# Grouped-query attention: the projections of the following sequence made between the attention groups of the sequence in hand

## The chip, the cores and the metric

The kernel runs on one core of a Trainium2 chip. The metric is the device time of one execution in microseconds (us): 7177.83 us for the kernel before, the median of three runs (7176.45 to 7178.78).

## What is computed

The program is a small two-layer network over x of shape [8, 256, 256] (8 sequences of 256 tokens, 256 channels), in float32. Its stages are a recurrent attention (RWKV7), a feed-forward block with masked attention, a gated linear recurrence, that feed-forward block again, a delta-rule attention with 16 heads, a mixture of experts, **grouped-query attention**, and the mixture of experts again. Only the grouped-query attention changes:

```python
h = layernorm(x)                                   # 8 x 256 x 256
q = h @ Wq + bq                                    # 32 heads of 8
k = h @ Wk + bk ; v = h @ Wv + bv                  # 8 key/value heads of 8
for every head: p = softmax(q k^T / sqrt(8)) ; o = p v      # no mask, 256 x 256 scores
x = x + (o @ Wo + bo)
```

## The kernel before

Each stage is a function. It holds its tiles in SBUF, and one program for each engine (`pe`, `act`, `dve`, `pool`, `sp`), written in the order in which that engine does it. Engines wait for each other by semaphores (`wait_ge`, `then_inc`). A `Block` ends when all its engines have ended it; `s.barrier()` follows, and clears the stage's semaphores. `nc.Fori` is a loop that the engines run on the chip, with one copy of its body in the instruction stream.

`gqa` (L1102) first makes the layer norm of all 2048 tokens into `xn_all` (L1133 to L1149); GpSimd's multiply (L140) is its last step, and VectorE clears `v` beside it (L1148). Then `Fori(0, BATCH)` (L1152) runs eight times, one sequence each, and every pass has these parts:

- **Projections.** TensorE makes the queries (8 tiles of 128x256, L1158, PSUM banks 1 to 4), the keys (2 tiles, L1164, bank 5) and the values (L1170, L1172, bank 6). ScalarE adds the bias and copies queries and keys to `qt` and `kt` (L1187, L1192), VectorE spreads the values into `v` (L1203). TensorE waits for all three before the first scores (`attn_pe`, from L806).
- **Attention.** 16 groups of 4 heads' tiles, each for one half of the queries. TensorE in round i: `scores(i + 1)` (L770, one of two pairs of PSUM banks, 1 to 4), `turn(i - 1)`, which transposes the probabilities (L781, banks 5 and 6), and `pv(i - 2)` (L792, bank 7). ScalarE: four exponentials of group i (L832), then the copy of the transposed probabilities (L842). VectorE: the row maximum of the scores of group i (L897), its negation (L898), then the reciprocal (L868) and the multiply that normalise group i - 1 (L871).
- **End.** VectorE copies the result (L913), TensorE multiplies by `wo` (L1178), VectorE adds bias and residual (L1209), and the barrier follows.

A matmul of float32 stands in the trace as two records, each with a weight load of its own; a transpose as one.

Of the kernel before, what the change touches and what calls it, by code (L numbers as in the profile page):

```python
# [23 lines left out]
P = 128  # L24
# [686 lines left out]
GH = 4  # L711
# [14 lines left out]
def attn_setup(s, tiles, head, scale, masked, k_tile, v_slots, v_at):  # L726
# [5 lines left out]
    n.qt = s.sb("qt", [P, tiles, SEQ])  # L732
    n.kt = s.sb("kt", [P, k_tile(tiles - 1) + 1, SEQ])
    n.v = s.sb("v", [P, QT, v_slots, 32])
# [12 lines left out]
    return n  # L747
# [13 lines left out]
def attn_pe(nc, g, n, pe):  # L761
    def scores(i):
        q, t = n.groups[i]
        if i >= 2:
            pe.wait_ge(n.masked_ready if n.masked else n.probs_ready, i - 1)
        w = key_tiles(n, q) * P
        for j in (0, 2, 1, 3):
            tile, row = head_at(t, j)
            rows = slice(32 * row, 32 * row + 32)
            last = nc.tensor.matmul(n.ps_s[i % 2][:, j, 0:w], n.qt[rows, tile, q * P:(q + 1) * P],  # L770
                                    n.kt[rows, n.k_tile(tile), 0:w], start=True, stop=True)
        last.then_inc(n.scores_ready, 1)
# [11 lines left out]
    def pv(i):  # L784
# [4 lines left out]
        for c in range(key_tiles(n, q)):  # L789
            for j in range(GH):  # L790
                out = n.ps_ot[32 * j:32 * j + 32, t // per, q * P:(q + 1) * P]
                last = nc.tensor.matmul(out, n.v[:, c, n.v_at(t, j)], n.pt[:, i % 2, j, c],  # L792
                                        start=t % per == 0 and c == 0,
                                        stop=t % per == per - 1 and c == key_tiles(n, q) - 1)
# [10 lines left out]
    pe.wait_ge(n.q_in_sb, 1)  # L805
    pe.wait_ge(n.k_in_sb, 1)  # L806
    pe.wait_ge(n.v_in_sb, 1)
    scores(0)
    for i in range(len(n.groups) + 2):
# [4 lines left out]
        if i >= 2:  # L814
            pv(i - 2)
        if i == n.tiles + 3 and n.masked:
            shares(0)
# [4 lines left out]
def attn_act(nc, n, act):  # L822
# [26 lines left out]
    for i in range(len(n.groups) + 1):  # L849
        if i < len(n.groups):  # L850
            exps(i)
        if i >= 1:
            copy_out(i - 1)
        if i == n.tiles + 4 and n.masked:
# [5 lines left out]
def attn_dve(nc, n, dve):  # L860
# [23 lines left out]
    for i, (q, t) in enumerate(n.groups):  # L884
# [15 lines left out]
        if i >= 1 and not n.masked:  # L900
            normalise(i - 1)
        if i == n.tiles + 1 and n.masked:
# [22 lines left out]
def ffn(nc, g, a):  # L925
    with ExitStack() as ctx:
# [28 lines left out]
        with nc.Block() as block:  # L955
# [29 lines left out]
            def _(dve):  # L985
# [13 lines left out]
                nc.vector.memset(t_.v[:], 0.0).then_inc(t_.v_clear, 1)  # L999
# [3 lines left out]
        with nc.Fori(0, BATCH) as b:  # L1003
            with nc.Block() as block:
                @block.tensor
                def _(pe):
# [11 lines left out]
                    last.then_inc(t_.v_ready, 1)  # L1018
                    attn_pe(nc, g, t_, pe)
# [32 lines left out]
                def _(act):  # L1052
                    for ready, ps, dst, done in ((t_.q_ready, ps_q, t_.qt, t_.q_in_sb),
                                                 (t_.k_ready, ps_k, t_.kt, t_.k_in_sb)):
# [12 lines left out]
                def _(dve):  # L1067
# [3 lines left out]
                    v_to = t_.v[:].rearrange("p c (a r rp) (j d) -> p c a r rp j d", r=2, rp=2, j=2)  # L1071
# [30 lines left out]
def gqa(nc, g, a):  # L1102

    with ExitStack() as ctx:
# [7 lines left out]
        n = ln_setup(s)  # L1112
        t_ = attn_setup(s, GQ_T, GQ_HEAD, float(GQ_HEAD) ** -0.5, False, lambda t: t // REP, 2 * KV_HEADS,
                        lambda t, j: 2 * (t // REP * GH + head_at(t, j)[1]) + t % REP // 2)
        m = s.names("x_seq_ready w_load q_half out_ready x_done ones_ready")
        attn_banks(g, t_)
        HALF = GQ_T // 2
        ps_q = [psum(g, 1 + 2 * i, HALF * SEQ).rearrange("p (t n) -> p t n", t=HALF) for i in range(2)]
        ps_k = psum(g, 5, KV_T * SEQ).rearrange("p (t n) -> p t n", t=KV_T)
        ps_v = psum(g, 6, QT * kv).rearrange("p (t n) -> p t n", t=QT)  # L1120
        ps_y = [psum(g, 1, SEQ), psum(g, 2, SEQ)]

        with nc.Block() as block:
# [21 lines left out]
            def _(dve):  # L1145
                ln_dve(nc, g, n, dve)
                nc.vector.memset(ones[:], 1.0)
                nc.vector.memset(t_.v[:], 0.0).then_inc(m.ones_ready, 1)  # L1148
                dve.wait_ge(m.ones_ready, 1)  # L1149
        s.barrier()  # L1150

        with nc.Fori(0, BATCH) as b:  # L1152
            with nc.Block() as block:
                @block.tensor
                def _(pe):
                    for t in range(GQ_T):
                        for k in range(KD):
                            last = nc.tensor.matmul(ps_q[t // HALF][:, t % HALF], wq[:, k, t * P:(t + 1) * P],  # L1158
                                                    n.xn[:, k, seq_cols(b)], start=k == 0, stop=k == KD - 1)
                        if t % HALF == HALF - 1:  # L1160
                            last.then_inc(t_.q_ready, 1)
                    for t in range(KV_T):
                        for k in range(KD):
                            last = nc.tensor.matmul(ps_k[:, t], wk[:, k, t * P:(t + 1) * P], n.xn[:, k, seq_cols(b)],  # L1164
                                                    start=k == 0, stop=k == KD - 1)
                    last.then_inc(t_.k_ready, 1)
                    pe.wait_ge(m.x_seq_ready, 1)
                    for t in range(QT):
                        for k in range(KD):
                            nc.tensor.matmul(ps_v[:, t], x_seq[:, k, t * P:(t + 1) * P], wv[:, k],  # L1170
                                             start=k == 0, stop=False)
                        last = nc.tensor.matmul(ps_v[:, t], ones[:], bv[:], start=False, stop=True)  # L1172
                    last.then_inc(t_.v_ready, 1)
                    attn_pe(nc, g, t_, pe)
                    pe.wait_ge(t_.ot_in_sb, 1)
                    for t in range(KD):
                        for k in range(KD):
                            last = nc.tensor.matmul(ps_y[t], wo[:, k, t * P:(t + 1) * P], t_.ot[:, k],  # L1178
                                                    start=k == 0, stop=k == KD - 1)
                    last.then_inc(m.out_ready, 1)  # L1180

                @block.scalar
                def _(act):
                    for t in range(GQ_T):
                        if t % HALF == 0:
                            act.wait_ge(t_.q_ready, t // HALF + 1)
                        last = nc.scalar.activation(t_.qt[:, t], ps_q[t // HALF][:, t % HALF], ACT.Identity,  # L1187
                                                    bias=bq[:, t:t + 1])
                    last.then_inc(t_.q_in_sb, 1)
                    act.wait_ge(t_.k_ready, 1)  # L1190
                    for t in range(KV_T):
                        last = nc.scalar.activation(t_.kt[:, t], ps_k[:, t], ACT.Identity, bias=bk[:, t:t + 1])  # L1192
                    last.then_inc(t_.k_in_sb, 1)
                    attn_act(nc, t_, act)

                @block.vector
                def _(dve):
                    nc.vector.tensor_copy(x_seq[:], n.xn[:, :, seq_cols(b)]).then_inc(m.x_seq_ready, 1)
                    dve.wait_ge(t_.v_ready, 1)
                    v_from = ps_v.rearrange("p c (a r rp d) -> p c a r rp d", r=2, rp=2, d=GQ_HEAD)  # L1200
                    v_to = t_.v[:].rearrange("p c (a r rp i) (j d) -> p c a r rp i j d", r=2, rp=2, i=2, j=4)
                    for c, half, i in product(range(QT), range(2), range(2)):
                        last = nc.vector.tensor_copy(v_to[:, c, :, half, :, i, 2 * i + half], v_from[:, c, :, half])  # L1203
                    last.then_inc(t_.v_in_sb, 1)
                    attn_dve(nc, t_, dve)
                    dve.wait_ge(m.out_ready, 1)
                    for k in range(KD):
                        xs = g.x_all[:, k, seq_cols(b)]
                        nc.vector.scalar_tensor_tensor(xs, ps_y[k], bo[:, k:k + 1], xs, ALU.add,  # L1209
                                                       ALU.add).then_inc(m.x_done, 1)  # L1210
                    dve.wait_ge(m.x_done, KD)
            s.barrier()
# [1693 lines left out]
```

## Time and profile before

| | |
|---|---|
| median of the runs | 7177.83 us |
| the profiled execution, its own time | 7175.3 us |
| its span, first to last instruction | 7173.5 us |
| mean granted TensorE clock | 0.868 of full speed |
| grouped-query attention, the eight passes | from 5943.1 to 6544.3 us |
| one pass | 75.1 us |

The times below are microseconds from the start of the span. The page describes the whole program, in which this stage is one twelfth; the stage is read by windows cut at its own instructions. The passes are alike, so one of them, from 6018.8 to 6093.9 us, is read closely.

### The profile page before, as it was taken

How to read it: one execution, taken by the hardware profiler on the slowest of the kernel's cores; microseconds unless marked ns; L12 is line 12 of the kernel's file. 1: busy time of each engine (PE TensorE's matmuls, PEld its weight loads, DVE VectorE, ACT ScalarE, POOL GpSimd, SP SyncE). 2: the span in 40 equal slices, each digit the busy share in tenths (PEclk: the TensorE clock that was granted, in tenths of full speed). 3: DMA queues.
4: the chain of work that ended last, by engine and by line, in shares of the span. 5: the costliest groups of instructions: out<-in, count | busy, mean ns of one | idle time of the engine just before them, and what ended most of it. 6: DMA issues, size and time to landing. Idle time of an engine off the chain costs nothing. (4 is left out here: it accounts for less than half of the span.)

```text
span 7173.5 us, 125898 instructions
## 1 busy us (share of the span) xinstructions
PE 5933.8 (83%) x52932; PEld 3888.6 (54%) x52932; DVE 3095.2 (43%) x4518; ACT 2846.2 (40%) x5150; POOL 2242.8 (31%) x1577
## 2 busy tenths in 40 slices
PE   6777688955698868888888888888889998888999
PEld 5666466634466535555555555555644445665444
DVE  4333423232432335565555656555632115564211
ACT  2222334343343435455455454554531116674111
POOL 3333200000100025566655656555522220001222
PEclk8777788877788879889898889988889998889999
DMA  0000000000000000000000000000021110002111
GB/s 25 2 2 2 29 0 0 0 13 0 29 0 0 2 20 15 20 17 15 15 15 15 22 15 15 15 15 22 15 74 42 41 36 10 0 0 75 42 42 46
DMA packets 60565, 136.47 MB, mean 19 GB/s; under 512 B 11638, under 2 KB 24054, under 8 KB 58842
## 3 DMA queue, kind: packets, MB, share of 16 engines
q1 hardware_dynamic: 60122, 129.79, 5.4%
q8 instruction: 372, 6.09, 0.3%
q14 instruction: 71, 0.58, 0.0%
HBM read 127.26 MB, written 2.50 MB: 18 GB/s over the span
## 5 line engine op out<-in xcount | busy, mean ns | idle before, releaser
L569 PE MATMUL ps<-moe_xn_all,moe_w 128*128 128x512 f32 x1792 | 810.3, 595 | 0.0
L1399 PE MATMUL ps<-kda_xn_all,kda_w_front 128*128 128x512 f32 x808 | 464.4, 728 | 130.0 <-ACT kda_cv L1438 103.6
L569 PEld LDWEIGHTS ps<-moe_xn_all,moe_w 128*128 128x128 f32 x1792 | 341.2, 191 | 424.0 <-issue 423.3
L1688 POOL TENSOR_TENSOR kda_g<-kda_g,kda_f 128x512 f32<-128x512 f32 x225 | 422.9, 1879 | 458.1 <-DVE kda_rows L1680 451.4
L682 DVE TENSOR_TENSOR moe_h<-moe_silu,ps 128x512 f32<-128x512 f32 x224 | 154.0, 687 | 936.0 <-ACT moe_silu L624 928.6
L1511 DVE SCALAR_TENSOR_TENSOR kda_cv<-kda_pre,kda_w_front,kda_cv 128x1024 f32<-128x1024 f32 x297 | 542.2, 1826 | 3.6
L624 ACT ACTIVATE moe_silu<-ps 128x512 f32<-128x512 f32 x224 | 133.7, 597 | 986.5 <-PE ps L569 986.4
L525 POOL TENSOR_TENSOR moe_h<-moe_h,moe_cb 128x512 f32<-128x512 f32 x176 | 233.7, 1328 | 696.4 <-DVE moe_h L682 696.4
L579 PE MATMUL ps<-moe_h,moe_w 128*128 128x512 f32 x896 | 420.4, 592 | 0.0
L1680 POOL TENSOR_TENSOR kda_rows<-kda_q,kda_f 128x512 f32<-128x512 f32 x225 | 322.4, 1433 | 243.3 <-remote 215.2
L1399 PEld LDWEIGHTS ps<-kda_xn_all,kda_w_front 128*128 128x128 f32 x808 | 178.9, 233 | 346.4 <-issue 200.4
L1770 PE MATMUL ps<-kda_x_sb,kda_t 64*64 64x32 f32 x5120 | 310.1, 220 | 0.0
L1689 POOL TENSOR_TENSOR kda_f<-kda_f 128x512 f32<-128x512 f32 x225 | 303.7, 1350 | 17.7
L1773 PE MATMUL ps<-kda_t,kda_x_sb 64*64 64x32 f32 x5120 | 306.8, 219 | 0.0
L1709 POOL TENSOR_TENSOR kda_cols<-kda_col,kda_g 128x512 f32<-128x512 f32 x192 | 296.3, 1543 | 0.0
L579 PEld LDWEIGHTS ps<-moe_h,moe_w 128*128 128x128 f32 x896 | 170.2, 190 | 214.3 <-issue 213.3
L1770 PEld LDWEIGHTS ps<-kda_x_sb,kda_t 64*64 64x64 f32 x5120 | 255.1, 134 | 41.2 <-issue 29.6
L1941 DVE TENSOR_TENSOR kda_t<-ps,kda_t 128x256 f32<-128x256 f32 x320 | 120.9, 419 | 361.9 <-PE ps L1773 360.8
L832 ACT ACTIVATE ffn_p<-ffn_sm,ffn_nmax 128x256 f32<-128x256 f32 (+1 forms) x512 | 225.7, 442 | 101.7 <-DVE ffn_nmax L898 101.7
L1773 PEld LDWEIGHTS ps<-kda_t,kda_x_sb 64*64 64x64 f32 x5120 | 256.0, 135 | 0.0
L832 ACT ACTIVATE gqa_p<-ps,gqa_nmax 128x256 f32<-128x256 f32 x512 | 236.1, 490 | 36.1 <-DVE gqa_nmax L898 36.1
L1761 PE MATMUL ps<-kda_t,kda_lt 64*64 64x64 f32 x5120 | 183.7, 221 | 75.3 <-DVE kda_lt L1920 75.3
(504 smaller groups left out, 12830.9 us busy)
## 6 DMA issues: line engine op xcount, KB each, us to landing
kda_col<-kda_beta SPq DMA_DIRECT2D x34, 512.0 KB, 4.2
moe_w<-in_Mw SPq DMA_DIRECT2D x6, 2816.0 KB, 19.8
moe_cb<-kda_beta SPq DMA_DIRECT2D x64, 256.0 KB, 3.1
kda_w_front<-in_Kw SPq DMA_DIRECT2D x34, 455.0 KB, 4.9
moe_cb<-kda_beta SPq DMA_DIRECT2D x32, 224.0 KB, 2.9
kda_w_out<-in_Kw SPq DMA_DIRECT2D x32, 192.5 KB, 4.8
moe_cb<-kda_beta SPq DMA_DIRECT2D x32, 192.0 KB, 2.8
moe_cb<-kda_beta SPq DMA_DIRECT2D x32, 160.0 KB, 2.7
```

The lines of the kernel that those rows point to most:

```text
L525: nc.gpsimd.tensor_tensor(h[:, u % H_BUFS], h0[:, u % H_BUFS], scale, ALU.mult).then_inc(m.h_ready, 1)
L569: last = nc.tensor.matmul(ps_gu[u % 2][r], w13[:, k, i, r], n.xn[:, k, cols(c)], start=k == 0, stop=k == KD - 1)
L579: last = nc.tensor.matmul(ps_y[d], w2[:, i, d * P:(d + 1) * P], h[:, u % H_BUFS], start=i == 0, stop=i == M_TILES - 1)
L832: last = nc.scalar.activation(n.p[:, i % 3, j, 0:w], src, ACT.Exp, scale=n.scale, bias=n.nmax[:, i % 2, j:j + 1], accum_out=n.sums[:, q, s ...
L1399: last = nc.tensor.matmul(psum(g, FRONT + hf, BANK), w[:, at:at + P], xn_all[:, k, bass.ds(quad * QUAD + hf * BANK, BANK)], start=k == 0, ...
L1511: ins = nc.vector.scalar_tensor_tensor(cv[i % 2][:], pre[i % 2][:, :, j:j + SEQ], w_vec(w, K_CONV + i * CONV + j), cv[i % 2][:], ALU.mult, ...
L1680: engine.tensor_tensor(out, halves((o.a, o.q)[r][:], h, 1), halves(o.f[:], h, 1), ALU.mult).then_inc(done, 1)
L1688: step(nc.gpsimd.tensor_tensor(halves(decay_g[:], h, 0), halves(decay_g[:], h, 0), second_total, ALU.mult))
L1689: step(nc.gpsimd.tensor_tensor(halves(o.f[:], h, 1), halves(o.f[:], h, 1), first_total, ALU.mult))
L1709: nc.gpsimd.tensor_tensor(halves(cols_s[l % 2][:], h, 0), halves(cur.col[:], h, 0), halves(decay_g[:], h, 0), ALU.mult).then_inc(n.scaled, 1)
L1770: nc.tensor.matmul(ps_dt[b, at, 0], t[b, at, 1], own_half(x_sb[b, at], h, 0), start=True, stop=True)
L1773: last = nc.tensor.matmul(ps_dt[b, at, 1], x_sb[b, at], own_half(t[b, at, 1], h, 1), start=True, stop=True)
```

## The change

The loop runs over pairs of sequences, with two blocks in its body, one for each sequence. Sequence 0 is projected in a block of its own ahead of the loop. Each block does the attention of its own sequence from `qt[own]`, `kt[own]`, `v[own]`, and makes the projections of the following one into the other copy. A hook `between(i)` is called at the end of round i on each engine. All new projections use PSUM bank 0: five units of two tiles (queries four, keys one), a unit waiting until ScalarE has emptied the bank of the one ahead, then the values. TensorE makes the units in rounds 3, 5, 7, 9, 11 and the values in round 13; ScalarE copies the units out in rounds 4, 6, 8, 10, 12; VectorE copies the tokens for the values in round 2 and the values in round 14. `xn_all` gets 256 columns of zeros at its end, which the last sequence's block projects. The waits that `attn_pe` began with are gone from this stage; `attn_pe`, `attn_act` and `attn_dve` of the feed-forward blocks call an empty hook.

```diff
 def attn_pe(nc, g, n, pe, own=0, between=nothing_between):
...
-    pe.wait_ge(n.q_in_sb, 1)
-    pe.wait_ge(n.k_in_sb, 1)
-    pe.wait_ge(n.v_in_sb, 1)
     scores(0)
     for i in range(len(n.groups) + 2):
         if i + 1 < len(n.groups):
...
         if i >= 2:
             pv(i - 2)
+        between(i)
...
-        ps_q = [psum(g, 1 + 2 * i, HALF * SEQ).rearrange("p (t n) -> p t n", t=HALF) for i in range(2)]
-        ps_k = psum(g, 5, KV_T * SEQ).rearrange("p (t n) -> p t n", t=KV_T)
-        ps_v = psum(g, 6, QT * kv).rearrange("p (t n) -> p t n", t=QT)
+        ps_pair = psum(g, 0, 2 * SEQ).rearrange("p (t n) -> p t n", t=2)
+        ps_v = psum(g, 0, QT * kv).rearrange("p (t n) -> p t n", t=QT)
+        Q_PAIRS, PAIRS = GQ_T // 2, (GQ_T + KV_T) // 2
...
-                nc.vector.memset(t_.v[:], 0.0).then_inc(m.ones_ready, 1)
+                nc.vector.memset(xn_all[:, :, TOKENS:], 0.0).then_inc(m.ones_ready, 1)
+                for v in t_.v:
+                    nc.vector.memset(v[:], 0.0).then_inc(m.ones_ready, 1)
...
+        def pair_pe(pe, cols, u):
+            if u > 0:
+                pe.wait_ge(m.pair_in_sb, u)
+            w, tile = (wq, 2 * u) if u < Q_PAIRS else (wk, 2 * (u - Q_PAIRS))
+            for t in range(2):
+                for k in range(KD):
+                    last = nc.tensor.matmul(ps_pair[:, t], w[:, k, (tile + t) * P:(tile + t + 1) * P],
+                                            xn_all[:, k, cols], start=k == 0, stop=k == KD - 1)
+            last.then_inc(m.pair_ready, 1)
...
+        def values_pe(pe):
+            pe.wait_ge(m.pair_in_sb, PAIRS)
+            pe.wait_ge(m.x_seq_ready, 1)
...
+        def pair_act(act, dst, u):
+            act.wait_ge(m.pair_ready, u + 1)
+            to, bias, tile = (t_.qt[dst], bq, 2 * u) if u < Q_PAIRS else (t_.kt[dst], bk, 2 * (u - Q_PAIRS))
+            for t in range(2):
+                last = nc.scalar.activation(to[:, tile + t], ps_pair[:, t], ACT.Identity,
+                                            bias=bias[:, tile + t:tile + t + 1])
+            last.then_inc(m.pair_in_sb, 1)
...
+        with nc.Block() as block:
+            first = slice(0, SEQ)
+            @block.tensor
+            def _(pe):
+                for u in range(PAIRS):
+                    pair_pe(pe, first, u)
+                values_pe(pe)
...
+        s.barrier()
-        with nc.Fori(0, BATCH) as b:
-            with nc.Block() as block:
+        with nc.Fori(0, BATCH // 2) as two:
+            for own in range(2):
+                at = two * (2 * SEQ) + own * SEQ
+                cur, nxt = bass.ds(at, SEQ), bass.ds(at + SEQ, SEQ)
+                with nc.Block() as block:
+                    @block.tensor
+                    def _(pe):
+                        def next_seq(i):
+                            if i % 2 == 1 and 3 <= i < 3 + 2 * PAIRS:
+                                pair_pe(pe, nxt, (i - 3) // 2)
+                            if i == 3 + 2 * PAIRS:
+                                values_pe(pe)
+                        attn_pe(nc, g, t_, pe, own, next_seq)
...
+                    @block.scalar
+                    def _(act):
+                        def next_seq(i):
+                            if i % 2 == 0 and 4 <= i < 4 + 2 * PAIRS:
+                                pair_act(act, 1 - own, (i - 4) // 2)
...
+                    @block.vector
+                    def _(dve):
+                        def next_seq(i):
+                            if i == 2:
+                                seq_dve(nxt)
+                            if i == 4 + 2 * PAIRS:
+                                values_dve(dve, 1 - own)
```

## Rows read from the trace of the kernel before

**Rows 1.** The page, part 1: busy us (share of the span) xinstructions of each engine.

```profile
PE 5933.8 (83%) x52932; PEld 3888.6 (54%) x52932; DVE 3095.2 (43%) x4518; ACT 2846.2 (40%) x5150; POOL 2242.8 (31%) x1577
```

**Rows 2.** Busy time by stretch, of one pass; then the first pass's start.

```profile
core 0: us, PE busy (x) PEld busy (x) DVE busy (x) ACT busy (x) POOL busy (x), PEclk, DMA share, GB/s
6018.80:6093.85 75.05, 63.05 (x572) 46.08 (x572) 45.70 (x76) 49.05 (x154) 0.00 (x0) 0.86 0.00 0
6019.31:6032.65 13.34, 12.28 (x53) 10.43 (x53) 1.11 (x9) 3.97 (x10) 0.00 (x0) 0.87 0.00 0
6032.65:6051.30 18.65, 15.20 (x98) 10.49 (x100) 12.18 (x18) 10.64 (x36) 0.00 (x0) 0.54 0.00 0
6051.30:6088.67 37.37, 33.58 (x416) 23.71 (x414) 30.65 (x46) 34.44 (x109) 0.00 (x0) 1.00 0.00 0
6088.67:6094.15 5.48, 1.99 (x8) 1.44 (x8) 1.57 (x4) 0.00 (x0) 0.00 (x0) 1.00 0.00 0
...
5943.10:5949.00 5.90, 5.90 (x14) 4.73 (x15) 0.43 (x1) 0.00 (x0) 0.00 (x0) 0.51 0.00 1
```

**Rows 3.** The waits from 5900 to 6560 us: total us, times, longest.

```profile
ACT gqa_qt L1187 <- PE ps L1158: 111.0, 16, 12.9
```

**Rows 4.** Instructions in order of time, projections: start, us, engine, line, what, [idle before].

```profile
6028.00 1.89 PE L1164 MATMUL ps<-gqa_xn_all,gqa_wk 128*128 x8
6029.73 0.55 PE L1170 MATMUL ps<-gqa_wv,gqa_x_seq 128*128 128x64 f32 x4
...
6029.93 0.84 ACT L1192 ACTIVATE gqa_kt<-ps,gqa_bk 128x256 f32<-128x256 f32 x2 [0.16 <-PE ps L1164]
...
6031.63 0.87 DVE L1203 COPY gqa_v<-ps 128x32 f32<-128x32 f32 x8 [12.07 <-PE ps L1172]
...
6032.65 1.16 PE L770 MATMUL ps<-gqa_kt,gqa_qt 32*128 32x256 f32 x16 [1.06 <-DVE gqa_v L1203]
```

**Rows 5.** Instructions in order of time, two rounds of attention at full clock.

```profile
6059.45 1.23 DVE L871 TENSOR_TENSOR gqa_p<-gqa_p,gqa_rsum 128x1024 f32<-128x1024 f32 x1
...
6060.73 1.09 PE L781 MATMUL ps<-net_ident,gqa_p 128*128 128x128 f32 x8 [0.20 <-DVE gqa_p L871]
...
6061.75 0.64 PE L792 MATMUL ps<-gqa_pt,gqa_v 128*32 128x128 f32 x16
...
6062.33 1.13 PE L770 MATMUL ps<-gqa_kt,gqa_qt 32*128 32x256 f32 x8
...
6063.51 1.23 DVE L897 TENSOR_REDUCE gqa_nmax<-ps 128x4 f32<-128x1024 f32 x1 [0.15 <-PE ps L770]
...
6065.05 1.22 DVE L871 TENSOR_TENSOR gqa_p<-gqa_p,gqa_rsum 128x1024 f32<-128x1024 f32 x1
```

**Rows 6.** TensorE in order of time, attention at half clock.

```profile
6041.17 2.08 PE L770 MATMUL ps<-gqa_kt,gqa_qt 32*128 32x256 f32 x8
...
6046.09 2.08 PE L770 MATMUL ps<-gqa_kt,gqa_qt 32*128 32x256 f32 x8
...
6050.00 1.08 PE L792 MATMUL ps<-gqa_pt,gqa_v 128*32 128x128 f32 x16
```

**Rows 7.** Loop branches of PE's sequencer, three loops: ns min/median/max, first and last start.

```profile
L2717 PEldq COMPARE_BRANCH  x8: 79/3644/4407, 135.6 to 780.4; - x8
...
L2105 PEldq COMPARE_BRANCH  x8: 83/3494/3649, 2963.0 to 5256.5; - x8
...
L1152 PEldq COMPARE_BRANCH  x8: 83/214/250, 6018.8 to 6544.3; - x8
```

**Rows 8.** Busy time by stretch, one pass of the loop of L2717 (RWKV7).

```profile
227.39:319.66 92.27, 71.74 (x1196) 58.98 (x1196) 35.67 (x73) 21.98 (x35) 35.45 (x35) 0.78 0.01 2
```

**Rows 9.** DMA queues, 227.4 to 780 us; then 6023 to 6544 us.

```profile
q8 instruction: 68, 1.11, 0.8%
...
DMA packets 0, 0.00 MB, mean 0 GB/s; under 512 B 0, under 2 KB 0, under 8 KB 0
```

**Rows 10.** Instructions in order of time, the end of the layer norm.

```profile
5939.09 2.34 POOL L140 TENSOR_TENSOR gqa_xn_all<-gqa_xn_all,gqa_ln_rstd_b 128x1024 f32<-128x1024 f32 x1 [0.63 <-DVE gqa_ln_rstd_b L232]
5939.30 0.91 DVE L1148 MEMSET gqa_v<- 128x1024 f32 x1 [0.16 <-issue]
```

More of the change, by code:

```diff
@@ L723, in head_rows, with nothing_between, attn_setup @@
     return [head_at(per * o + k, j) for o in range(KD) for j in range(GH) for k in range(per)]
-def attn_setup(s, tiles, head, scale, masked, k_tile, v_slots, v_at):
+def nothing_between(i):
+    pass
+def attn_setup(s, tiles, head, scale, masked, k_tile, v_slots, v_at, copies=1):
     n = s.names("q_ready k_ready v_ready q_in_sb k_in_sb v_in_sb v_clear scores_ready masked_ready nmax_ready "
@@ L731, in attn_setup @@
     n.tiles, n.head, n.scale, n.masked, n.k_tile, n.v_at = tiles, head, scale, masked, k_tile, v_at
-    n.qt = s.sb("qt", [P, tiles, SEQ])
-    n.kt = s.sb("kt", [P, k_tile(tiles - 1) + 1, SEQ])
-    n.v = s.sb("v", [P, QT, v_slots, 32])
+    n.qt = [s.sb(f"qt{i}", [P, tiles, SEQ]) for i in range(copies)]
+    n.kt = [s.sb(f"kt{i}", [P, k_tile(tiles - 1) + 1, SEQ]) for i in range(copies)]
+    n.v = [s.sb(f"v{i}", [P, QT, v_slots, 32]) for i in range(copies)]
     if masked:
@@ L758, in key_tiles, with attn_pe @@
     return q + 1 if n.masked else QT
-def attn_pe(nc, g, n, pe):
+def attn_pe(nc, g, n, pe, own=0, between=nothing_between):
     def scores(i):
@@ L769, in scores @@
             rows = slice(32 * row, 32 * row + 32)
-            last = nc.tensor.matmul(n.ps_s[i % 2][:, j, 0:w], n.qt[rows, tile, q * P:(q + 1) * P],
-                                    n.kt[rows, n.k_tile(tile), 0:w], start=True, stop=True)
+            last = nc.tensor.matmul(n.ps_s[i % 2][:, j, 0:w], n.qt[own][rows, tile, q * P:(q + 1) * P],
+                                    n.kt[own][rows, n.k_tile(tile), 0:w], start=True, stop=True)
         last.then_inc(n.scores_ready, 1)
@@ L791, in pv @@
                 out = n.ps_ot[32 * j:32 * j + 32, t // per, q * P:(q + 1) * P]
-                last = nc.tensor.matmul(out, n.v[:, c, n.v_at(t, j)], n.pt[:, i % 2, j, c],
+                last = nc.tensor.matmul(out, n.v[own][:, c, n.v_at(t, j)], n.pt[:, i % 2, j, c],
                                         start=t % per == 0 and c == 0,
@@ L819, in attn_pe, with attn_act @@
         shares(1)
-def attn_act(nc, n, act):
+def attn_act(nc, n, act, between=nothing_between):
     def exps(i):
@@ L853, in attn_act @@
             copy_out(i - 1)
+        between(i)
         if i == n.tiles + 4 and n.masked:
@@ L857, in attn_act, with attn_dve @@
         shares(1)
-def attn_dve(nc, n, dve):
+def attn_dve(nc, n, dve, between=nothing_between):
     step = Chain(dve, n.at_step)
@@ L901, in attn_dve @@
             normalise(i - 1)
+        between(i)
         if i == n.tiles + 1 and n.masked:
@@ L1018, in _ @@
                     last.then_inc(t_.v_ready, 1)
+                    pe.wait_ge(t_.q_in_sb, 1)
+                    pe.wait_ge(t_.k_in_sb, 1)
+                    pe.wait_ge(t_.v_in_sb, 1)
                     attn_pe(nc, g, t_, pe)
@@ L1052, in _ @@
                 def _(act):
-                    for ready, ps, dst, done in ((t_.q_ready, ps_q, t_.qt, t_.q_in_sb),
-                                                 (t_.k_ready, ps_k, t_.kt, t_.k_in_sb)):
+                    for ready, ps, dst, done in ((t_.q_ready, ps_q, t_.qt[0], t_.q_in_sb),
+                                                 (t_.k_ready, ps_k, t_.kt[0], t_.k_in_sb)):
                         act.wait_ge(ready, 1)
@@ L1147, in _ @@
                 nc.vector.memset(ones[:], 1.0)
-                nc.vector.memset(t_.v[:], 0.0).then_inc(m.ones_ready, 1)
-                dve.wait_ge(m.ones_ready, 1)
+                nc.vector.memset(xn_all[:, :, TOKENS:], 0.0).then_inc(m.ones_ready, 1)
+                for v in t_.v:
+                    nc.vector.memset(v[:], 0.0).then_inc(m.ones_ready, 1)
+                dve.wait_ge(m.ones_ready, 3)
         s.barrier()
-        with nc.Fori(0, BATCH) as b:
-            with nc.Block() as block:
-                @block.tensor
-                def _(pe):
-                    for t in range(GQ_T):
-                        for k in range(KD):
[L1158 to L1212, printed above, removed]
@@ new lines, in pair_pe @@
+        def pair_pe(pe, cols, u):
[10 more added lines that the diff above has]
+            pe.wait_ge(m.x_seq_ready, 1)
+            for t in range(QT):
+                for k in range(KD):
+                    nc.tensor.matmul(ps_v[:, t], x_seq[:, k, t * P:(t + 1) * P], wv[:, k], start=k == 0, stop=False)
+                last = nc.tensor.matmul(ps_v[:, t], ones[:], bv[:], start=False, stop=True)
+            last.then_inc(t_.v_ready, 1)
@@ new lines, in values_dve @@
+        def values_dve(dve, dst):
+            dve.wait_ge(t_.v_ready, 1)
+            v_from = ps_v.rearrange("p c (a r rp d) -> p c a r rp d", r=2, rp=2, d=GQ_HEAD)
+            v_to = t_.v[dst][:].rearrange("p c (a r rp i) (j d) -> p c a r rp i j d", r=2, rp=2, i=2, j=4)
+            for c, half, i in product(range(QT), range(2), range(2)):
+                last = nc.vector.tensor_copy(v_to[:, c, :, half, :, i, 2 * i + half], v_from[:, c, :, half])
+            last.then_inc(t_.v_in_sb, 1)
+        with nc.Block() as block:
[7 more added lines that the diff above has]
+            def _(act):
+                for u in range(PAIRS):
+                    pair_act(act, 0, u)
+                act.wait_ge(m.pair_in_sb, PAIRS)
+            @block.vector
+            def _(dve):
+                seq_dve(first)
+                values_dve(dve, 0)
+                dve.wait_ge(t_.v_in_sb, 1)
```

34 lines of the change are left out of this document (28 added, 6 removed).

## The prediction

> **What bounds the kernel now.** The page comes first: TensorE is busy for 83% of the span, twice as much as any other engine [rows 1]. That is a mean over eight stages, and says nothing of this one. So the second view is busy time by stretch, cut at this stage's own instructions [rows 2]. One pass takes 75.05 us, eight make the stage's 601 us, and it has four parts: 13.34 us of projections, 18.65 us of attention in which the granted clock is 0.54 (half speed, 1.2 GHz, nearly throughout), 37.37 us of attention at 2.4 GHz, and 5.48 us of output and barrier. The reader is to see that in the first part VectorE and ScalarE together work 5.1 us of 13.34, and that in the third TensorE works 33.6, VectorE 30.7 and ScalarE 34.4 of 37.4 us: none of the three is much above the others. The list of waits says the same of the first part: ScalarE stood 111.0 us in 16 waits for the query matmuls [rows 3].
>
> The third view is the order of time. In the projections TensorE works without a gap until the values, then waits 1.06 us for VectorE's copy [rows 4]. At full clock, rounds of attention are bound by a chain through two engines [rows 5]: the multiply of VectorE starts at 6059.45, transposes at 6060.73 (1.28 later), `pv` at 6061.75 (1.02), scores at 6062.33 (0.58), the maximum at 6063.51 (1.18), the next multiply but one at 6065.05 (1.54). That is 5.60 us for two rounds, 2.80 a round; two such chains interleave. At half clock TensorE is the bound by itself: from scores to scores 4.92 us [rows 6].
>
> **The change, part by part.**
>
> *Removed: the serial projections.* 13.34 us a pass [rows 2], eight times: 106.7 us.
>
> *Added: the same matmuls between the rounds.* Two key tiles, 8 records, took 1.89 us at full clock [rows 4]; a unit of two tiles is the same work, so five are 9.45. The values ran from 6029.73 to the copy at 6031.63, 1.90, less the handover 1.86. Sum 11.31 us a pass. Which cover is there? A unit stands in TensorE's queue behind `pv` and ahead of scores, inside the chain of 5.60 us, and behind it are queued the scores of the next group but one, for which VectorE and then ScalarE wait. So the chain becomes 7.49 us, and the unit is paid in full. The units come in every second round, always in the same of the two interleaved chains, and the other can't run ahead in an in-order queue. From below: TensorE is idle 37.37 - 33.58 = 3.8 us of a pass's fast part [rows 2]; if the units fill all of it, the cost is 7.5. From above: a unit at half clock costs 3.4 us (14 records in 5.90 us, 8 of them [rows 2]). The first unit follows `pv(1)`, which started at 6050.00, 17.4 us after the first scores, and ran about 1 us more [rows 4, 6]; the clock rose at 6051.3 [rows 2]. So the units fall behind the slow stretch, if that keeps its length and its place behind the first scores. I take 11.3, in range 7.5 to 14.4 (two units at half clock).
>
> ScalarE's 0.84 us a unit (two copies [rows 4]) and VectorE's 0.87 for the values come in the time that TensorE's unit opens: ScalarE idles 2.9 us of the fast part and gets 1.89 more for each 0.84, and the value copies lie beside scores (1.18 us to the maximum [rows 5]). The waits that are added (`pair_in_sb` on TensorE) are for copies of the round ahead. Cost 0; uncovered it would be 0.84 x 5 + 0.87 = 5.1.
>
> Eight passes: (11.31 - 13.34) x 8 = -16.2 us.
>
> *Added: sequence 0 on its own.* One bank, so a unit and its copy-out alternate: at full clock 5 x (1.89 + 0.84 + 0.2 handovers, estimated from the 0.16 and 0.1 us gaps of rows 4) = 14.7, values 1.86 and copy 0.97, and a barrier, 1.8 (5.48 less 1.99 of matmuls and 1.57 of VectorE leaves 1.9 [rows 2]): 19.3 us. At half clock units 3.4 and values 3.3: 28.3. TensorE came into the first pass at half clock and kept it for the first 5.9 us of unbroken matmuls [rows 2]; with gaps of 1 us between units it should rise later. I take 24.
>
> *Moved: the loop's back edge.* The body of the loop becomes two passes long. One pass is 572 matmul and 572 weight-load records of TensorE [rows 2]; its back edge cost PE's sequencer 0.21 us, and no instruction packet moved from the second pass to the last [rows 7, 9]. The RWKV7 loop has 1196 + 1196 records in a pass [rows 8]: there the same branch took 3.64 us in the median, 4.41 at most, the delta-rule loop's 3.49, and 68 instruction packets moved in six passes, about eleven in each [rows 7, 9]: the body is loaded anew every time. The new body has 2 x 1144 = 2288. Between 1144 and 2392, 2288 is close to the upper row, so I take that: three back edges at 3.63 - 0.21 = 3.4 us, 10.3 us, with bounds 0 and 3 x 4.2 = 12.6. All of it is exposed, because scores are the first work of a block and everybody waits for them. The four boundaries inside the body have no branch (0.3 us each), -1.2.
>
> [...]
>
> *Setup.* VectorE clears a second `v` (0.91) and the zero columns (about 0.45) beside GpSimd's multiply of 2.34 us, of which 1.1 is now used [rows 10]: 0.1.
>
> **Sum.** -16.2 + 24 + 10.3 - 1.2 + 0.1 = +17.0 us. The profiled execution took 7175.3 us, so 7192; the median of the runs is 2.5 above it: 7195.
>
> **The rivals.**
>
> *A. The longer body still fits in the instruction memory.* The edge costs 0.2 as now. For it: 2288 lies under 2392, and no row shows the border. Against: it is 96% of a body that is reloaded. 7195 - 10.3 = 7185.
>
> *B. Faster: TensorE's idle time takes the units in.* If the 3.8 us of idle time in the fast part are filled, a pass is shorter by 5.8 instead of 2.0: 30 us less, 7165, faster than before. It decides from 4.2 us a pass gained, that is 2.2 of the 3.8 filled. For it: the idle time is there, and the chain has waits for VectorE in it. Against: the unit is inside the chain, and TensorE's own round is 1.08 + 1.02 + 0.58 = 2.68 of 2.80 us [rows 5], which leaves 0.12 a round; much of the 3.8 lies in the last rounds, where no unit is.
>
> *C. The clock moves.* Every us of half clock in the attention costs 1 - 2.80/4.92 = 0.43 us. C1: the slow stretch gets 7 us shorter, now that dense matmuls stand where light ones stood: 3.0 x 8 = 24 less, 7171. C2: it gets 7 us longer, since nothing dense runs ahead of the scores and the back edge leaves TensorE idle for 3 us more: 7219. Against both: the fall comes with the idle time after the first scores, which stays, and the first unit comes where the clock rises now.
>
> *D. The change doesn't do what it says.* If a unit's copy is late, TensorE stands at the next unit; two rounds (7.49 us) lie between them, ScalarE's copy needs 0.84. I give this nothing by itself.
>
> **How the numbers follow.** Forecast (7183 to 7207 with its own bounds) 0.56; A 0.10; B 0.08; C1 0.12; C2 0.14. The range that leaves 2 in 10 out: 7172 to 7216. What a measurement of this kernel can tell from no change is 0.2%, 14.4 us: below 7163.5 is faster, above 7192.2 slower. Forecast: 6 in 10 of it above 7192 (0.34), and nearly all of C2 (0.14), a tenth of A and a little of the others: slower 0.52. Faster is part of B and of C1: 0.07. The same: 0.41.
>
> **What would show it.** A pass's span between barriers near 73.0 us (75.05 - 2.0); in rounds with a unit, two rounds in about 7.5 us instead of 5.6; PE's branch of this loop at 3.4 to 4.4 us with 9 or more instruction packets in each later pass of the body; the block of sequence 0 at 19 to 28 us; the slow stretch at 17 us, with the first unit at its end. I am wrong if two rounds with a unit take under 6.5 us, if the branch stays at 0.21, or if the granted clock in the passes leaves 0.80 to 0.90 (0.86 now).

## The result, and the profile after

The changed kernel takes 7190.08 us in the median of 13 runs (7182.65 to 7200.03), the one before 7176.49 us in 13 runs (7169.62 to 7182.94). The ratio is 1.0019, with a 95% interval of 1.0010 to 1.0027: the change makes the kernel slower by 0.1 to 0.3%, 13.6 us in the medians. 7195 had been predicted, with a range of 7172 to 7216. The prediction held that nothing under 14.4 us could be told from no change; with 13 runs of each kernel the interval excludes no change at 13.6.

The page says little, as before: TensorE's share is the same 83%, with 52 more matmul records, those of the zero columns [rows 1].

```profile
PE 5937.8 (83%) x52984; PEld 3881.7 (54%) x52984; DVE 3100.0 (43%) x4529; ACT 2849.0 (40%) x5160; POOL 2242.6 (31%) x1577
```

The second view answers to [rows 2]: busy time by stretch, cut at the stage's own instructions. The columns are those of [rows 2]; the rows are the block of sequence 0 with its barrier, one pass from first scores to the result's copy, two stretches of it at half and at full clock, and the way from the copy over the loop's back edge to the next scores. A slow stretch is one in which the granted clock is at the lower of its two levels (1.2 GHz, PEclk 0.50).

```profile
5951.18:5973.56 22.38, 15.27 (x52) 10.98 (x53) 1.30 (x9) 4.20 (x10) 0.00 (x0) 0.81 0.00 1
6192.74:6260.01 67.27, 59.99 (x564) 42.85 (x564) 44.45 (x73) 48.79 (x154) 0.00 (x0) 0.87 0.01 1
...
6194.60:6211.70 17.10, 14.34 (x82) 9.95 (x83) 11.84 (x19) 10.96 (x38) 0.00 (x0) 0.50 0.01 1
6211.70:6260.01 48.31, 44.49 (x468) 32.13 (x466) 31.93 (x54) 37.84 (x117) 0.00 (x0) 1.00 0.01 2
6260.01:6268.85 8.84, 2.00 (x9) 1.47 (x9) 1.57 (x3) 0.00 (x0) 0.00 (x0) 0.86 0.01 4
```

The reader is to see three things. The serial part of 13.34 us is gone, but the attention takes 67.27 us where it took 18.65 + 37.37 = 56.02. The slow stretch has the length it had, 17.1 us; in it TensorE is busy 14.3 us and yet runs at half clock. And the boundary with the branch, from the copy to the next work of TensorE, is 8.84 us long, 5.71 before (6013.60 to 6019.31).

The third view is the order of time, two rounds with a unit; it answers to [rows 5].

```profile
6233.94 1.99 PE L1168 MATMUL ps<-gqa_xn_all,gqa_wq 128*128 x8
...
6235.87 1.13 PE L774 MATMUL ps<-gqa_kt,gqa_qt 32*128 32x256 f32 x8
...
6237.05 1.23 DVE L900 TENSOR_REDUCE gqa_nmax<-ps 128x4 f32<-128x1024 f32 x1 [1.47 <-PE ps L774]
...
6238.59 1.23 DVE L874 TENSOR_TENSOR gqa_p<-gqa_p,gqa_rsum 128x1024 f32<-128x1024 f32 x1
6238.98 0.83 ACT L1185 ACTIVATE gqa_qt<-ps,gqa_bq 128x256 f32<-128x256 f32 x2
...
6239.87 1.09 PE L785 MATMUL ps<-net_ident,gqa_p 128*128 128x128 f32 x8 [0.21 <-DVE gqa_p L874]
...
6240.89 0.64 PE L796 MATMUL ps<-gqa_pt,gqa_v 128*32 128x128 f32 x16
...
6241.47 1.78 PE L1168 MATMUL ps<-gqa_xn_all,gqa_wk 128*128 x7
```

From unit to unit it is 7.53 us, where two rounds took 5.60. VectorE now waits 1.47 us for the scores behind the unit, 0.15 before. ScalarE's copies (L1185) aren't free: VectorE's reciprocal at 6241.67 waits 0.52 us for the exponentials behind one. But TensorE works at the next unit meanwhile (6241.47 on) and doesn't wait for it. The chain is the one that was priced: unit, scores, maximum, multiply, transposes, `pv`, next unit.

PE's branch of the loop answers to [rows 7], the instruction packets (6118 to 6558 us, three later bodies) to [rows 9]:

```profile
L1222 PEldq COMPARE_BRANCH  x4: 82/3564/3787, 6117.7 to 6559.1; - x4
```

```profile
q8 instruction: 33, 0.54, 0.5%
```

### The profile page after: what moved, and what is told of

Read it like the earlier page. It is cut to its first block and busy times, and to the rows that moved or that the text cites. A ratio compares the mean times of both kernels' runs of the same rounds, so it can differ in the third digit from the quotient of the medians.

```text
span 7191.1 us, 126017 instructions
## 1 busy us (share of the span) xinstructions
PE 5937.8 (83%) x52984; PEld 3881.7 (54%) x52984; DVE 3100.0 (43%) x4529; ACT 2849.0 (40%) x5160; POOL 2242.6 (31%) x1577
```

## Experiments

All times of the stage below are read in each run's own profile, from the start of the first projection matmul to the start of the last residual: 599.4 us before, 606.0 after. Its parts are the start (first projection to first scores), eight attentions (scores to the result's copy), and the boundaries between them. Without the clock's share a part comes out alike within about 1 us from profile to profile; a single time of the whole kernel doesn't resolve that. Where two stretches of attention are compared, their slow stretches must be compared too: the prediction prices each us of one at 0.43 us.

### The changed kernel again

No edit.

> The changed kernel itself once more, for a second profile. Its profiled execution started this stage 8 us later than the one before (5951 to 5943), in stages that the change doesn't touch. If that is chance, this one starts anywhere from 5940 to 5951 as the other runs did, and the stage takes 606 us again to within 3 us; if the change moved the other stages, it starts at 5951 again.

It started the stage at 5945.4 us, and the stage took 610.1 us: 4.1 more than in the first profile (3 were allowed), with a slow stretch of 23.9 us in the place of one of 17.1, and one of 17.1 in the place of one of 13.7. In the first profile it was 5951.2; in the eleven others it was 5939.6 to 5949.3, and the latest of these starts is that of a kernel which does all work ahead of the loop as the kernel before does (two passes in the body, below). So the 8 us ahead of the stage in the first profile aren't put down to the change. The stage itself is longer by 6.6 and 10.7 us in the two profiles. The part behind it took 633.9 and 633.5 us in them and 631.1 before. Both have 3.4 us at half clock within 3 us behind the stage, the profile before has none there; the rest of the 2.6 us wasn't located. It isn't in the changed code by itself: with the loop written out (below) this part took 631.0.

### Units left out

```diff
-                        attn_pe(nc, g, t_, pe, own, next_seq)
+                        attn_pe(nc, g, t_, pe)
-                        attn_act(nc, t_, act, next_seq)
-                        act.wait_ge(m.pair_in_sb, PAIRS)
+                        attn_act(nc, t_, act)
-                        attn_dve(nc, t_, dve, next_seq)
-                        dve.wait_ge(t_.v_in_sb, 1)
+                        attn_dve(nc, t_, dve)
```

> The changed kernel without any projection in the loop: all eight passes attend with the queries, keys and values of sequence 0 (the projections of sequences 1 to 7 are left out). It measures what the units, their copies and the value work cost where they stand. From first scores to the result's copy a pass took 66.5 us in the mean after (65.3 to 68.1) and 56.0 before. My theory: the cost is TensorE's 11.3 us in the chain, a pass falls to 55.5 or less in this part. The measured passes came out 1.1 us shorter than my sum had them; if the units are paid in full, this run shows passes of 55.2 and the missing us in the clock's place; if they were partly hidden (10.4 or less each pass), passes of 56.0. The body is 1,960 records or so of TensorE: if the border is at 2,048, the branch is back at 0.21 us; if it lies lower, it stays at 3.4 to 3.8.

The attentions took 53.6 to 56.2 us, 54.7 in the mean; 66.5 in the mean in the kernel after. The difference is 11.8 us a pass, 11.3 had been summed. About one of the 11.8 is clock: the half-clock time inside the eight attentions is 108 us here and 128 after. At equal slow stretches of 17.1 us, one pass here took 56.2 and three after took 67.0 to 67.3. So units and values cost 10.8 to 11.1 us by themselves, nearly in full. One of the passes with a shorter slow stretch, scores to copy:

```profile
6149.34:6203.03 53.69, 46.28 (x512) 32.68 (x512) 42.75 (x65) 45.04 (x144) 0.00 (x0) 0.90 0.01 1
```

The mean without units is 1.3 us under the 56.0 of before, at a granted clock of 0.88 in the mean here (0.90 in this pass) and 0.85 before: 28 us less of slow stretch in eight passes, at 0.43, are 1.5 us a pass. The branch took 3.38 to 3.67 us, although the body had lost its units; two passes of 2 x 520 records are 2080. So between 1144 and 2080 lies the border, and the 1,960 records of the expectation were miscounted. Records are matmuls and weight loads alone; waits for semaphores, some 18 a pass, come on top of them in every body.

### Units' matmuls twice

```diff
-            for t in range(2):
+            for t in (0, 1, 0, 1):
                 for k in range(KD):
                     last = nc.tensor.matmul(ps_pair[:, t], w[:, k, (tile + t) * P:(tile + t + 1) * P],
```

> The changed kernel with every unit's eight matmuls of TensorE made twice, into the same bank; ScalarE's copies stay as they are. My theory (a unit stands inside the chain of two rounds and is paid in full): each pass grows by 5 x 1.89 = 9.45 us and the block of sequence 0 by 5 x 1.9 to 3.4; two rounds with a unit take 7.5 + 1.9 = 9.4 us. Rival (part of the unit is covered by TensorE's idle time and ScalarE's copy is what counts): the second half isn't covered any better, but growth stays under 8 us a pass.

The attentions took 75.9 us in the mean, 9.4 more, and the start 29.9, 7.5 more. In the order of time one doubled unit reads:

```profile
6273.28 3.72 PE L1168 MATMUL ps<-gqa_xn_all,gqa_wk 128*128 x16
6276.93 1.13 PE L774 MATMUL ps<-gqa_kt,gqa_qt 32*128 32x256 f32 x8
```

3.65 us from unit to scores, 1.93 in the kernel after. Two rounds with such a unit took 9.25 us (6264.03 to 6273.28), 9.4 had been said. At equal slow stretches of 17.1 us the passes took 76.1 to 76.3 against 67.0 to 67.3, so 9.0 of the 9.4 us are the second halves and the rest is clock: of 9.45 us added, at most half a microsecond is covered. The rival of this run (under 8) falls. Rival B of the prediction wants 2.2 us a pass of the first halves covered, which this run can't see; the run without units refutes it, at 10.8 and more where B leaves 9.1.

### Two passes in the body, nothing else

```diff
-        with nc.Fori(0, BATCH) as b:
-            with nc.Block() as block:
+        with nc.Fori(0, BATCH // 2) as two:
+            for own in range(2):
+                cur = bass.ds(two * (2 * SEQ) + own * SEQ, SEQ)
+                with nc.Block() as block:
```

> The kernel before with one thing of the change alone: the loop's body holds two passes (Fori over 4, two blocks), and projections stay serial, as they were. Before, the stage took 601.3 us from its first projection to its last loop branch. My theory: TensorE's body of 2,288 records is loaded anew at each of three back edges; PE's branch takes 3.4 to 3.8 us instead of 0.21 (+10), the four boundaries without a branch save 0.4 us each and the four other edges' absence is in that: stage 601.3 + 10.3 - 1.6 = 610 us, with about nine instruction packets of PE in each later body. Rival (the edge is long for another reason, such as the larger bank of registers or the hooks): the branch stays at 0.21 and the stage at 600.

The branch did what was said, 3.41, 3.42 and 3.81 us. The stage did not: 598.7 us, not 8 or so above 599.4 but level. Busy time by stretch, from the copy to the next scores, shows why. First the kernel before:

```profile
6163.76:6182.74 18.98, 14.28 (x60) 11.88 (x61) 2.86 (x12) 3.97 (x10) 0.00 (x0) 0.91 0.00 0
```

Then this one, at a boundary inside the body and at a back edge:

```profile
6170.26:6187.11 16.85, 12.59 (x61) 10.72 (x61) 2.86 (x12) 3.97 (x10) 0.00 (x0) 1.00 0.00 0
```
```profile
6241.61:6264.61 23.00, 15.00 (x60) 12.42 (x61) 2.87 (x12) 3.97 (x10) 0.00 (x0) 0.85 0.01 3
```

Each back edge costs 4.0 us more, 12 in all: 3.3 in the branch, the rest at a clock of 0.85 where it was 0.91. Each boundary without a branch costs 2.1 less: 0.5 up to the first projection matmul, 5.20 us after the copy where it was 5.71, and the rest in the clock, which stays at 1.00 in the projections where it fell to 0.91. The attentions are 4 us shorter in sum, in slow stretches 7 us shorter in sum. So the load of the body is real and its branch costs what was forecast, and it was given back by the clock, which is why the stage's total hides it. The whole kernel took 7181.2 us in its one run, against 7174.1 for the kernel before beside it. That looks like the 8 us that were expected, but in this profile the stage starts 6.2 us later than before and is no longer, so it shows nothing.

### The loop written out

```diff
-        with nc.Fori(0, BATCH // 2) as two:
+        for two in range(BATCH // 2):
...
-                cur, nxt = bass.ds(at, SEQ), bass.ds(at + SEQ, SEQ)
+                cur, nxt = slice(at, at + SEQ), slice(at + SEQ, at + 2 * SEQ)
```

> The changed kernel with no loop: the eight blocks are written out, slices are constants. After, the stage took 607.9 us from its first projection unit to its last branch, with three back edges of 3.4 to 3.8 us. My theory: the load of instructions costs only at a taken branch, sequential loading is hidden, so the stage falls by 10 us to 597 and each boundary takes 5.2 us from the result's copy to the next scores. Rival: instructions that are run once each come late too, and stalls at block borders give the 10 us back: 608.

595.4 us to the last residual, 10.6 less than after (10 had been said), and every boundary 5.02 to 5.05 us long:

```profile
6249.01:6254.04 5.03, 2.00 (x9) 1.47 (x9) 1.57 (x3) 0.00 (x0) 0.00 (x0) 1.00 0.00 0
```

The seven boundaries are 13.0 us shorter in sum than after, 12.1 of it at the three that had the branch. The attentions took 66.8 us in the mean, 66.5 after, which takes 2.5 back; that the total agrees with the forecast so well is in part chance. 27 instruction packets moved during the last six passes, and no boundary waits for them: loading in sequence is hidden here, although every instruction is run once; only the taken branch waited.

### Sequence 0 into banks 1 to 6

```diff
+            own_q = [psum(g, 1 + 2 * i, GQ_T // 2 * SEQ).rearrange("p (t n) -> p t n", t=GQ_T // 2) for i in range(2)]
+            own_k = psum(g, 5, KV_T * SEQ).rearrange("p (t n) -> p t n", t=KV_T)
...
-                for u in range(PAIRS):
-                    pair_pe(pe, first, u)
+                for u in range(PAIRS):
+                    ps = own_q[u // 2][:, 2 * (u % 2):2 * (u % 2) + 2] if u < Q_PAIRS else own_k
...
```

> The changed kernel with sequence 0 projected as before the change, into banks 1 to 6 without waiting for the copies between units. After, it took 22.4 us from the first projection to the first scores, of which 13.4 us or more ran at half clock. My theory: 14.5 us as in the kernel before and a barrier of 1.9: 16.4, stage 606 to 600. Rival (the clock of the first pass is what the time hangs on, not the alternation): 20 or more.

```profile
5946.05:5961.38 15.33, 12.78 (x52) 10.79 (x53) 1.30 (x9) 4.20 (x10) 0.00 (x0) 0.83 0.00 1
```

15.3 us, against 22.4: the alternation of one bank costs 7 us, a third of it (15.27 - 12.78 = 2.5 us of TensorE's busy time) by half clock, the rest by waiting: in the kernel after, TensorE waits 0.93 us for ScalarE's copy behind each of the five units. By the granted clock (0.81, in the second view above), 8.5 of the 22.4 us were at half clock, not the 13.4 of the expectation. The stage took 602.5; the other half of the gain went to a slow stretch of 23.9 us in one pass.

### Units three rounds earlier

```diff
-                            if i % 2 == 1 and 3 <= i < 3 + 2 * PAIRS:
-                                pair_pe(pe, nxt, (i - 3) // 2)
-                            if i == 3 + 2 * PAIRS:
+                            if i % 2 == 0 and i < 2 * PAIRS:
+                                pair_pe(pe, nxt, i // 2)
+                            if i == 2 * PAIRS:
```

ScalarE's and VectorE's rounds are shifted alike.

> The changed kernel with the units three rounds earlier: TensorE's in rounds 0, 2, 4, 6, 8, values in round 10, ScalarE's and VectorE's shifted alike. TensorE idles 3.4 us after the first two score groups of each pass; the first unit falls in that idle time. Theory 1 (a unit costs what it takes in TensorE's chain): the first unit is hidden, 1.9 us a pass less; and the next two fall in the slow stretch, at 3.4 instead of 1.9 us each, +3.0, if the stretch stays at 17 us: stage 608 + 8 x 1.1 = 617. Theory 2 (dense work in the idle time keeps or brings back the clock): the slow stretch shrinks from 17 us to 10 or less, worth 0.43 us per us, and the stage falls to 608 - 8 x (1.9 + 3) = 569 or below. Granted clock of the passes tells them apart: 0.88 or 0.93 and more.

```profile
6168.82:6229.07 60.25, 55.43 (x564) 39.77 (x564) 44.34 (x74) 48.58 (x154) 0.00 (x0) 0.97 0.01 2
```

The stage took 563.6 us, 42 less than after, and the kernel 7141.0 in its one run, against 7174.1 for the kernel before beside it. The slow stretches went from 144 us of the stage to 53, and an attention runs at 0.95 to 1.00, 0.86 to 0.90 after. Theory 1 is off by 53 us. This run alone doesn't say how much is clock and how much is the first unit, hidden in idle time; the next two do.

### One unit that nobody reads, in the kernel before

```diff
         if i + 1 < len(n.groups):
             scores(i + 1)
+        if i == 0 and extra:
+            extra()
...
+                    def idle_work():
+                        for t in range(2):
+                            for k in range(KD):
+                                nc.tensor.matmul(ps_idle[:, t], wq[:, k, t * P:(t + 1) * P],
+                                                 n.xn[:, k, seq_cols(b)], start=k == 0, stop=k == KD - 1)
```

> The kernel before with one addition: after the scores of the first two groups of each pass, TensorE makes one unit (8 matmul records) into bank 0 that nobody reads, in the 3.5 us in which it stood idle. No work is moved or taken away. If the dense work in the idle time holds the clock by itself, the slow stretch of 17 us in each pass goes or shrinks to 7 us or less, and a pass falls by 4 to 7 us: stage 599.4 to 545 to 565 (first projection to last residual). If the gain of the run with early units came from hiding work and not from the clock, a pass stays at 75.1 and the stretch at 17 us.

561.1 us, 38 less than the kernel before, by added work alone; the whole kernel took 7133.4 us in its one run, against 7176.0 beside it. TensorE in order of time, the start of one pass; it answers to [rows 6]:

```profile
6234.43 2.10 PE L770 MATMUL ps<-gqa_kt,gqa_qt 32*128 32x256 f32 x16 [1.06 <-DVE gqa_v L1212]
6236.45 2.70 PE L1180 MATMUL ps<-gqa_xn_all,gqa_wq 128*128 x8
6239.95 1.13 PE L770 MATMUL ps<-gqa_kt,gqa_qt 32*128 32x256 f32 x8 [0.79 <-ACT gqa_p L834]
6241.42 1.09 PE L781 MATMUL ps<-net_ident,gqa_p 128*128 128x128 f32 x8 [0.34 <-DVE gqa_p L873]
6242.44 1.13 PE L770 MATMUL ps<-gqa_kt,gqa_qt 32*128 32x256 f32 x8
```

Before, the scores of the third group took 2.08 us, and so did each of the next two. Here they take 1.13: the added matmuls (L1180) lie in the idle time, the clock is back when the third scores begin, and an attention takes 50.8 to 51.7 us instead of 56.0. The added work doesn't keep the clock from falling: it fell at 6234.5, as the first scores began, and rose at 6237.9, within the added matmuls. What it does is end the slow stretch after 3.4 us instead of 17.1.

```profile
6164.88:6215.66 50.78, 46.35 (x520) 32.36 (x520) 43.22 (x64) 44.91 (x144) 0.00 (x0) 0.97 0.00 0
```

### The same, in the kernel after

```diff
                         def next_seq(i):
+                            if i == 0:
+                                idle_pe(first)
                             if i % 2 == 1 and 3 <= i < 3 + 2 * PAIRS:
```

> The changed kernel with the same addition as in the run before (one unit that nobody reads, made in the idle time after the first two score groups); the real units stay in rounds 3 to 11. It splits the 42 us that early units gained: clock, or first unit hidden. If the clock does it: the slow stretches shrink to 3 to 7 us a pass, and from first scores to the result's copy a pass takes 50.8 (the kernel before with idle work) plus 11.5 of units and values, 62.3 instead of 66.5: stage 606 to 572. If the place of the real first unit did most of it: 65 or more, 595 and above.

578.9 us; attentions of 62.0 to 64.2, 63.1 in the mean, slow stretches of 53 us in all, as with early units. 572 and 62.3 had been expected for the clock, 595 and 65 for the place of the unit. One pass, scores to copy:

```profile
6180.94:6243.07 62.13, 57.16 (x572) 41.08 (x572) 44.18 (x73) 48.61 (x154) 0.00 (x0) 0.97 0.01 2
```

The whole kernel took 7159.8 us in its one run, 7177.0 for the kernel before beside it. So of the 5.4 us a pass that early units gained (66.5 to 61.1), 3.4 are the clock, and 2.0 are the real first unit, hidden in the idle time (1.89 priced).

### The parts together

Early units, the loop written out, sequence 0 into banks 1 to 6, and no units in the last pass:

> Four parts together: units three rounds earlier, the eight passes written out (no back edge), sequence 0 projected into banks 1 to 6, and no units in the last pass. Worked out from the runs so far: 16.4 us to the first scores, seven passes of 61 us and boundaries of 5.03, a last pass of 55, and 3.4: 537 us from first projection to last residual, against 599.4 before and 606.0 after; time 7176.5 - 62 = 7114 us, 0.991 of before. If the parts don't add up because the clock falls in passes that held it, up to 7 us a pass are lost: 7160.

7113.35 us in the median of 5 runs (7110.19 to 7116.65), against 7175.95 for the kernel before beside them: ratio 0.9912, interval 0.9898 to 0.9925. The stage took 536.6 us, 537 had been worked out. It is 63 us faster than the kernel before, and 77 under the 7190.1 that the kernel after took in other runs. Seven passes have slow stretches of 0 to 6.8 us; the last one, which has no unit, has 17.1:

```profile
6418.24:6474.27 56.03, 48.76 (x512) 34.21 (x512) 42.85 (x64) 45.14 (x144) 0.00 (x0) 0.85 0.01 1
```

### And idle work in the last pass

```diff
-... nothing_between if at + SEQ == TOKENS else next_seq)
+... (lambda i: idle_pe(first) if i == 0 else None) if at + SEQ == TOKENS else next_seq)
```

> The combined kernel, and in its last pass, which has no units, one unit in round 0 that nobody reads. That pass took 56.0 us from first scores to the copy with a slow stretch of 17 us, where passes with a unit in round 0 held the clock. My theory: it falls to 51, stage 536.6 to 531.6, time 7113 to 7108 or a ratio of 0.9905. Rival: nothing that can be told from 0.9912.

```profile
6429.70:6480.49 50.79, 46.38 (x520) 32.52 (x520) 43.22 (x64) 44.91 (x144) 0.00 (x0) 0.97 0.01 2
```

The pass did fall from 56.0 to 50.8. But the pass ahead of it took 64.1 us where it had taken 60.2, with a slow stretch of 10.2 us, and the stage took 535.2 us, where 531.6 had been expected. The ratio of 0.9913 (0.9900 to 0.9927; 7117.2 us in the median of 5 runs) can't be told from 0.9912: no gain shown.

## Why the prediction was right, step by step

**Direction and size.** Slower, as forecast; +17.0 us summed, +13.6 measured on the whole kernel, +6.6 and +10.7 in the stage of the two profiles. In the stage the sum was 6 to 10 us too high; that the forecast for the whole came within 4 us is partly luck, since about 3 us came behind the stage, where the sum had nothing.

**The units are paid in full: right.** 7.53 us for two rounds (7.49 said); 11.8 us a pass by leaving them out, 10.8 to 11.1 at an equal slow stretch (11.3); 9.4 more when doubled, 9.0 at an equal slow stretch (9.45). Copies by ScalarE and VectorE cost TensorE nothing that shows. Rival B is refuted, and D didn't come about: TensorE waited for a unit's copy only in sequence 0's block. From first scores to the next first scores without the branch a pass took 71.6 us in the mean, 73.0 had been said.

**The back edge: right.** 3.70, 3.43 and 3.79 us of branch; the three boundaries are 10.0 us longer than before (10.3 said), and writing the loop out took 12.1 off them. Eleven instruction packets a body were moved, nine or more said. Rival A is refuted: the runs put the border above 1144 records and at or below 2080. By the Trainium skill (Runtime: NRT & Kernel Launch, section Instruction fetch mechanics) PE's instruction memory holds 2,048 instructions, which lies between the two. The same section has a taken branch wait when its target is outside a window of two blocks, 256 instructions each; the kernel before doesn't bear that out, for its branch goes back over 1144 records in 0.21 us.

**The block of sequence 0: right within its bounds.** 22.4 and 22.6 us, 24 said. The serial projections that it takes the place of cost 14.5 in the first pass, not 13.3.

**Boundaries inside the body.** 0.3 to 0.5 us less each (5.2 to 5.4 against 5.7), 0.3 said.

**The term that was mis-sized: an attention of 56.0 + 11.3 = 67.3 us.** It took 66.5 in the first profile, 67.0 in the second; eight times 0.8 is most of what the first sum has too much. Of these 6.5 us, 3.6 are the clock's (8.4 us less at half clock inside the attentions, at 0.43); the rest is the units, which cost 0.2 to 0.5 us a pass less than summed. The clock's step is "if that keeps its length and its place behind the first scores". The length was mostly kept, the place was not: behind a back edge the fall comes ahead of the first scores (6119.5, with scores at 6121.5), so that less of the slow stretch lies in the attention; of the eight, one was 13.7 us, one 20.5 and six 17.1. This is rival C1 in small, and no clean result of either kind: in the second profile one stretch was 23.9 us, and the half-clock time in the attentions was 137 us, as before. Nor does the fall come with the idle time after the first scores, as the prediction had it: behind a back edge it came ahead of that idle time, and with the idle time filled it came all the same in six of eight passes.

**What I had not weighed.** I took the slow stretch as given, priced at 0.43 us for each us of it, and let it stand. The runs show it as the largest term that could be moved: idle work takes it from 166 to 56 us of the stage before, and saves 38. The change left TensorE's idle time of 3.5 us at the start of each pass empty, and put the dense matmuls behind the slow stretch; three rounds earlier the same change makes the stage 36 us shorter than before instead of 7 longer. What starts a slow stretch in these passes stays open; what ends it early is shown. And this is where the gain went that one might expect of moving the projections: under an attention whose chain already holds TensorE, 13.3 us of projections became 10.4 to 10.9 us more of attention, and what that saves, and more, was spent on the block of sequence 0 and on the back edge.

## What to carry to other kernels

Work moved beside other work is hidden only where its engine is idle: read the chain of a round first, and if the engine that gets the work is in it, look for idle time at the start and end of the loop's body instead. Before doubling a loop's body, count its TensorE records and compare its branch with those of the longer loops in the same trace. And if a trace shows light matmuls at half clock behind a short idle time, a few dense matmuls in that idle time, useful or not, are a cheap test; here they saved 38 us of 599. Read the parts of the stage, each with its clock, and not the time of the whole kernel alone: the load of a body of two passes cost 12 us at its back edges and left no trace in the stage's total.

## What the runs showed of the hardware

- In this stage the slow stretch at the start of an attention lasted 14 to 24 us, while TensorE was busy with scores, transposes and `pv` (14.3 of 17.1 us). With eight dense records (2.70 us) in its idle time the clock was back after 3.4 to 6.8 us in nearly every pass. In the boundaries inside the body TensorE was busy 2.0 of 5.2 us, and the granted clock was 1.00.
- PE's loop branch took 0.21 to 0.25 us with a body of 1144 records and 3.3 to 4.4 us with 2080 to 2448, and the later bodies were then loaded again (33 packets in three bodies of the kernel after); the same code without a loop loaded 27 packets in six passes and waited for nothing.
- The length of a slow stretch changes from run to run (13.7 to 23.9 us in the kernel after), so the same pass of the same kernel differed by up to 2.7 us between two executions (65.7 and 68.4 us), and the attentions of the kernel after lie from 65.3 to 68.4 us.
